# Sending each token's rows to their experts batch by batch, with scattered rows in place of gathered ones

## The reference, cut to what matters

```
logits = x @ gate_w.T                                   # 2048 x 64
topv, topi = jax.lax.top_k(logits, 8)
rw = jax.nn.softmax(topv)
W = jnp.zeros((N, E)).at[jnp.arange(N)[:, None], topi].set(rw)
gu = jnp.einsum('nh,eih->nei', x, gu_w)                 # gu_w 64 x 128 x 256
gate, up = gu[..., :64], gu[..., 64:]
inter_w = silu(gate) * up * W[:, :, None]
out = jnp.einsum('nei,ehi->nh', inter_w, dp_w)          # dp_w 64 x 256 x 64
out = out + sigmoid(x @ sh_gate1_w.T) * shared_expert(x)
```

## Time and profile before

| | |
|---|---|
| median of 3 runs | 1198.72 (1197.88 to 1201.56) |
| the profiled execution | 1203.47, its span 1201.7 |
| busy, PE / DVE / ACT / POOL | 907.1 / 869.8 / 567.8 / 520.3 |
| mean granted clock of TensorE | 0.895 |
| attention of layer 0 ends (last sum) | 143.55 |
| first gather for a unit, start of the last | 206.66, 446.72 |
| first and last gather of the return | 462.39, 630.09 |
| first work of the next block | 639.53 |

### The profile page before, as it was taken

The page is one execution under the profiler, slowest core; times in us unless marked ns, Lnnn a source line. Parts: engine busy times, 40 slices in busy tenths (PEclk is TensorE's granted clock), DMA queues, the critical chain, the costliest instruction groups (busy, mean ns, idle before and its releaser), DMA issues. The chain is left out here.

```text
span 1201.7 us, 16894 instructions
## 1 busy us (share of the span) xinstructions
PE 907.1 (75%) x5172; PEld 581.4 (48%) x5172; DVE 869.8 (72%) x2535; ACT 567.8 (47%) x1243; POOL 520.3 (43%) x532
## 2 busy tenths in 40 slices
PE   6899976888888884000007989999988899999887
PEld 5766744666666663000004433333322467688565
DVE  6467887599989873566445888878887569777465
ACT  3322267566666662000004366777768543434553
POOL 3100048777777764777774431111112144453000
PEclk9989985899999997555557999999999999999899
DMA  5060161677767765333332622222211300110001
GB/s 160 1 278 19 38 158 26 187 212 209 211 205 211 220 206 180 103 98 97 103 94 87 214 84 72 72 72 72 72 19 27 118 27 28 52 53 1 1 27 45
DMA packets 74522, 124.97 MB, mean 104 GB/s; under 512 B 12282, under 2 KB 52288, under 8 KB 73024
## 3 DMA queue, kind: packets, MB, share of 16 engines
q1 hardware_dynamic: 58944, 81.80, 22.3%
q0 software_dynamic: 15360, 41.96, 12.5%
q10 hardware_dynamic: 128, 0.13, 0.1%
HBM read 83.80 MB, written 35.66 MB: 99 GB/s over the span
## 5 line engine op out<-in xcount | busy, mean ns | idle before, releaser
L2026 DVE CUSTOM_DVE_ANT_0 masked<-ps,causal 128x128 f32<-128x128 f32 (+7 forms) x256 | 181.1, 755 | 40.7 <-PE ps L1825 39.7
L1539 POOL DMA_INDIRECT h_t<-modulated_rows,ga_rows x192 | 182.8, 952 | 60.8 <-issue 55.2
L145 PE MATMUL ps<-consts,xn 128*128 128x128 f32 x128 | 20.1, 308 | 177.1 <-PEq L78 104.2
L1551 POOL DMA_INDIRECT big<-expert_rows,slot x128 | 126.0, 984 | 55.2 <-issue 40.5
L2006 ACT ACTIVATE xn<-ps 128x512 f32<-128x512 f32 (+3 forms) x256 | 111.7, 511 | 43.6 <-PE ps L1847 42.7
L1458 DVE SCALAR_TENSOR_TENSOR xn<-big,weights,xn 128x256 f32<-128x256 f32 x128 | 62.5, 488 | 84.4 <-DMA big<-expert_rows,slot 80.4
L151 ACT ACTIVATE h_t<-ps,modc 128x512 f32<-128x512 f32 x24 | 17.4, 778 | 192.3 <-PE ps L145 97.9
L1130 PE MATMUL ps<-h_t,xn 128*128 128x128 f32 x768 | 104.9, 281 | 0.0
L145 PEld LDWEIGHTS ps<-consts,xn 128*128 128x128 f32 x128 | 16.8, 160 | 182.0 <-issue 109.9
L1130 PEld LDWEIGHTS ps<-h_t,xn 128*128 128x128 f32 x768 | 96.5, 197 | 0.9 <-issue 0.9
L1118 PE MATMUL ps<-consts,h_t 128*128 128x128 f32 x384 | 64.5, 292 | 35.9 <-DMA h_t<-modulated_rows,ga_rows 35.5
(11 more groups left out here) (321 smaller groups left out, 2184.4 us busy)
## 6 DMA issues: line engine op xcount, KB each, us to landing
expert_rows<-h_t SPq DMA_DIRECT2D x96, 256.0 KB, 2.6
qk<-qk_parts SPq DMA_DIRECT2D x72, 128.0 KB, 2.7
big<-in_gu SPq DMA_DIRECT2D x8, 1024.0 KB, 11.2
qk_parts<-parts SPq DMA_DIRECT2D x16, 384.0 KB, 2.6
raw<-in_mlp SPq DMA_DIRECT2D x16, 384.0 KB, 3.1
room<-in_down SPq DMA_DIRECT2D x4, 1024.0 KB, 10.7
h_t<-modulated_rows,ga_rows POOLq DMA_INDIRECT x192
h_t<-qk_parts SPq DMA_DIRECT2D x24, 128.0 KB, 2.7
```

The costliest lines, as they stand in the source:

```text
L1539: nc.gpsimd.indirect_dma_start(xg[:, u % 4, i, :], None, row_dram, bass.IndirectOffsetOnAxis(ap=idxg[:, 2 * u + i:2 * u + i + 1].bitcast(U ...
L1551: nc.gpsimd.indirect_dma_start(yg[:, t % 2, k, :], None, y_dram, bass.IndirectOffsetOnAxis(ap=slots[:, n:n + 1].bitcast(U32), axis=0))\
L2026: nc.vector.tensor_tensor_reduce(masked[:, at % 2, 0:k], ps[:, bank:bank + (k + GW - 1) // GW, :] .rearrange("p a n -> p (a n)")[:, 0:k], ...
```

## The change

- The capacity is now counted for each batch: 127 tiles, so 64 units a batch and 128 in all, where 96 were.
- Batch 0 is normalised, routed and given its slots inside batch 1's attention, at the tiles t = 8 to 12. TensorE's scores of t = 12 and t = 13 are no longer issued one tile ahead; those of 13 wait for the slots' keys.
- The list, its one-hot matrices and the gathers of L1539 go. POOL scatters instead (`send`): for each tile of tokens 8 indirect DMAs write the 128 rows from SBUF into their slots in `dispatched_rows`. A unit's 256 rows are then consecutive, and SP loads them with one plain DMA.
- Slots that no token has must hold finite numbers. SP fills `dispatched_rows` beforehand with 2 times 16 stores of 1 MB (`fill`), the first 16 in the projection block, the others in the attention.
- ACT takes over half of the unit's eviction, and the shared expert's output of batch 0.
- The rows of batch 0 are fetched and added while batch 1's units run (`combine_part`, 3 parts in 2 units); the return after the last unit has 8 tiles.

```diff
-SLOTS = (T * TOPK + E0 * (P - 1)) // P
-UNITS0 = (SLOTS + 1) // 2
+SLOTS = (SEQ * TOPK + E0 * (P - 1)) // P
+UB = (SLOTS + 1) // 2
+UNITS0 = BATCH * UB
...
+            FILLS = UB * 2 * P * D // (P * 2 * P * TOPK)
+            def fill(engine, b, rows_from):
+                rows = sent_dram[b * UB * 2 * P:(b + 1) * UB * 2 * P, :].rearrange("(n p r) d -> n p (r d)", n=FILLS, p=P)
+                for n in range(FILLS):
+                    engine.dma_start(rows[n], rows_from).then_inc(s_void[b], 16)
...
+            nothing = sb(projecting, "nothing", [P, 2 * P * TOPK])
...
+                    sp.wait_ge(s_clean, 1)
+                    fill(sp, 0, nothing[:, :])
                     sp.wait_ge(s_modd, 6)
                     sp.dma_start(mod_dram.rearrange("w b d -> b w d"),
...
+                    sp.wait_ge(s_wgu, 16 * 7)
+                    fill(sp, 1, big[:, 0:2 * P * TOPK])
...
+                    for i in range(UNITS0 + 7):
+                        if i < UNITS0:
+                            if i % UB == 0:
+                                all_sent(sp, i // UB)
+                            if i == 0:
+                                sp.wait_ge(s_shs, NG)
+                            if i >= 4:
+                                sp.wait_ge(s_t, i - 3)
+                            sp.dma_start(xg[:, i % 4, :, :],
+                                         sent_dram[i * 2 * P:(i + 1) * 2 * P, :].rearrange("(i p) d -> p i d", p=P))\
+                                .then_inc(s_xg[i % 4], 16)
+                        u = i - 7
+                        if u >= 0:
+                            sp.wait_ge(s_ye, u + 1)
+                            sp.wait_ge(s_yea, u + 1)
+                            sp.dma_start(y_dram[u * 2 * P:(u + 1) * 2 * P, :].rearrange("(i p) d -> p i d", p=P),
+                                         ys[:, u % 2, :, :]).then_inc(s_yst[u % 2], 16)
...
+                        if t in (8, 10):
+                            turned((t - 8) // 2)
+                        if t in (9, 11):
+                            logits((t - 9) // 2)
+                        if t == 11:
+                            scores(12)
+                        if t == 12:
+                            pe.wait_ge(s_cst, 2)
+                            count(0)
+                            pe.wait_ge(s_q, 1)
+                            ranks(0, ps[:, 3, :].rearrange("p (t e) -> p t e", t=TB), 0, TB)
+                            pe.wait_ge(s_key, 1)
+                            scores(13)
...
-                            nc.vector.tensor_copy(ys[:, u % 2, :, :],
-                                                  ps[:, 4 + 2 * (u % 2):6 + 2 * (u % 2), 0:D]).then_inc(s_ye, 1)
+                            nc.vector.tensor_copy(ys[:, u % 2, 0, :], ps[:, 4 + 2 * (u % 2), 0:D]).then_inc(s_ye, 1)
...
+                        u = i - 3
+                        if u >= 0:
+                            act.wait_ge(s_d, u + 1)
+                            if u >= 2:
+                                act.wait_ge(s_yst[u % 2], 16 * (u // 2))
+                            nc.scalar.copy(ys[:, u % 2, 1, :], ps[:, 5 + 2 * (u % 2), 0:D]).then_inc(s_yea, 1)
...
+                        late = i - UB - COMBINE_AT
+                        if late >= 0:
+                            for n in range(min(3 * late // 2, TB * PARTS), min(3 * (late + 1) // 2, TB * PARTS)):
+                                combine_part(n)
...
+                    def send(t):
+                        if t >= 2:
+                            pool.wait_ge(s_sent[t % 2], SENT * (t // 2))
+                        for n in range(t * TOPK, (t + 1) * TOPK):
+                            nc.gpsimd.indirect_dma_start(
+                                sent_dram, bass.IndirectOffsetOnAxis(ap=slots[:, n:n + 1].bitcast(U32), axis=0),
+                                xn[:, t, :], None).then_inc(s_sent[t % 2], 16)
...
+                    for t in range(NT):
+                        if t % TB == 0:
+                            pool.wait_ge(s_slot, t // TB + 1)
+                            pool.wait_ge(s_void[t // TB], 16 * FILLS)
+                        send(t)
+                        if t in (0, 3):
+                            ln_pool(pool, 1, (GB + t // 3,))
```

More of the change, by code:

```diff
@@ L1040, in tiles_of, with count @@
                     def tiles_of(t, n):
                         return bc(m16[:, t, :], 1, n)
-                    def bank(n):
-                        return ps[:, n, :].rearrange("p (t e) -> p t e", t=TB)
-                    def within(n, first):
-                        return nc.tensor.matmul(bank(n), tri16[:, :], m16[:, n * TB:(n + 1) * TB, :],
-                                                start=first, stop=False)
-                    def before(n):
-                        for t in range(TB - 1):
-                            nc.tensor.matmul(bank(n)[:, t + 1:, :], ones16[:, :], tiles_of(n * TB + t, TB - 1 - t),
+                    def count(b):
+                        pe.wait_ge(s_m, 2 * b + 2)
+                        out = ps[0:E0, 5 if b else 3, 0:1]
+                        for t in range(b * TB, (b + 1) * TB):
+                            last = nc.tensor.matmul(out, m16[:, t, :], ones16[:, 0:1], start=t == b * TB,
+                                                    stop=t == (b + 1) * TB - 1)
+                        last.then_inc(s_cnt, 1)
@@ L1057, in before, with ranks @@
+                    def ranks(b, out, first, n):
+                        nc.tensor.matmul(out, tri16[:, :], m16[:, first:first + n, :], start=True, stop=False)
+                        for t in range(b * TB, first):
+                            nc.tensor.matmul(out, ones16[:, :], tiles_of(t, n), start=False, stop=False)
+                        for t in range(n - 1):
+                            nc.tensor.matmul(out[:, t + 1:, :], ones16[:, :], tiles_of(first + t, n - 1 - t),
                                              start=False, stop=False)
+                        nc.tensor.matmul(out, q16[:, b, :], bc(later16[:, :], 1, n), start=False,
+                                         stop=True).then_inc(s_rank, 1)
@@ L1097, in _ @@
+                    pe.wait_ge(s_pta, len(hi_blocks))
+                    count(1)
                     shared(2)
+                    pe.wait_ge(s_q, 2)
+                    ranks(1, ps[:, 4, :].rearrange("p (t e) -> p t e", t=TB), TB, TB)
                     shared(3)
+                    for b in range(BATCH):
+                        last = nc.tensor.matmul(ps[0:E0, 5, 1 + b:2 + b], tri16[0:E0, 0:E0], q16[:, b, 0:1], start=True,
+                                                stop=True)
@@ L1167, in copied @@
                         for c in range(KC):
-                            last = nc.scalar.copy(h_t[:, c, g * GW:(g + 1) * GW], ps[:, T_BANK[g] + c, :])
+                            last = nc.scalar.copy(h_t[:, c, g * GW:(g + 1) * GW], ps[:, T_BANK[g][c], :])
                         last.then_inc(s_h, 1)
@@ L1246, in _ @@
                     act.wait_ge(s_tail, 16)
-                    for i in range(UNITS0 + 1):
+                    for i in range(UNITS0 + 3):
                         u = i
@@ L1272, in _ @@
                     nc.scalar.activation(c_row, c_row, ACT.Silu).then_inc(s_mod1, 1)
+                    for t in range(TB + 2, NT):
+                        shared_out(t)
                     act.wait_ge(s_modr, 2)
```

457 lines of the change are left out of this document (206 added, 251 removed).

## The result

The changed kernel takes 1223.3 us (median of 4 runs, 1219.2 to 1230.0) where the kernel before takes 1200.1 in the same comparison: 1.020 of it, 95% interval 1.014 to 1.026. It is slower, outside the range that was predicted and on the other side of no change. Its profiled execution is of 1219.2 with a span of 1217.5, 15.8 longer than the span before. It is the shortest of the four; the median stands 4.1 above it.

What follows compares the result with a forecast made beforehand. POOL's indirect DMAs were taken to bound loop and return, DVE close behind in the loop. 77 more for loop and start, 86 less for the return, 3 for the ends: 6 saved, 1192 us, range 1171 to 1212.

Steps and rivals of the forecast that it cites:

- From the median: 1198.7 - 6: Final step: 6 saved, taken from the old kernel's median, whose profiled execution stood 4.8 above it; 1192.7, say 1192.
- Routing inside attention, 19: Batch 0's routing ahead of attention's tile 13 adds 19; slots at about 134.5, attention ending near 160.
- Sends: Batch 0's 64 scatters on POOL at 1.257 each, 80.4, plus 3 for two `rstd` and a wait; first turn at 223.
- Fills, 0: The first 16 stores of 1 MB in the projection block take 39, done at 56, hidden, costing 0.
- The loop, 304.8: Expert loop of 128 units, first to last turn, summed over three paces to 304.8; last turn at 528.
- I take 2.45: Pace per unit while POOL sends batch 1, between 2.22 from DVE and 2.68 from DMA: 30.6 units in 75.
- 2.17 with POOL idle: Pace per unit once POOL's sends end, where TensorE's 2.11 binds: 33.4 units, 72.5.
- DVE 2.34 without POOL, 2.59 beside it ... I take 2.48: Pace per unit of batch 1's units carrying 80 combine parts, each part 0.52: 53.3 units, 132.2.
- The return, 105.5 from last turn to next block: After the last unit: first fetch at 540, 63 fetches at 1.30, landing and last sum; next block at 633.5.
- Nothing behind it changes.: Everything after the next block's start, 639.53 before, was taken as unchanged, so that start served as yardstick.
- queues bind: Rival, 0.24: while POOL issues DMAs, `ys` stores land late and ACT and DVE wait for the two buffers; 1204.
- The working's own signs of being wrong: Forecast wrong if batch 0's slots stand after 145 or before 125, or the mean pace lies outside 2.3 to 2.5.

Runs made afterwards that it cites:

- e25: The changed kernel with batch 0's count, ranks and slots after attention's last tile, batch 1's rstd ahead of the sends: 1235.1 us, 1.0314 of the kernel before.
- e10: The changed kernel with one semaphore per batch for the sends, so no send waits for earlier ones: 1214.2 us, 1.0128 of the kernel before.
- e23: e19 plus a third `ys` buffer, and the shared expert's multiplication and batch 0's 64 weights on DVE ahead of the first unit: 1186.7 us, 0.988 of the kernel before.
- e26: The changed kernel with DVE's wait for a part moved to just before the next part: 1213.1 us, 1.0108 of the kernel before.
- e22: The changed kernel with only parts 0 and 9 of each tile's sum left in the loop: 1210.1 us, 1.0083 of the kernel before.
- e19: The changed kernel with the deferred part wait, one semaphore per batch, and ScalarE copying both tiles from unit 72 on: 1204.1 us, 1.0046 of the kernel before.

## Why the prediction was wrong, step by step

The working gave 1197.5 for the profiled execution (1203.5 less 6) and 1219.2 was measured, 21.7 more: 9.9 up to the first turn (forecast 223), 6.9 in the loop, under 1 in the return and 4.5 behind it, to rounding. The step "From the median: 1198.7 - 6" adds another 9. It supposed that the new profiled execution would stand 4.8 above its median too, and it stands 4.1 below; that is the spread of executions, which the working did not reckon with, and no cost of the change. No one step carries the 21.7. The largest is the price of a unit with parts, and it is the step that failed.

- *Routing inside attention, 19.* Slots were forecast at 134.5 and stand at 138.3. The attention's end moved from 143.6 to 165.2, by 21.7; by the working's own 19 it would be 162.5, where the text says "near 160". The mechanism is right, the size some 3 to 4 short. e25 shows that the step pays 13 in this kernel.
- *Sends.* 1.257 each was right (1.265). The sentence "64 sends are 80.4, two `rstd` and a wait for group 2's statistics 3" left out that a send waits for sends two tiles back: 5.3 at 188 us. The wait is in the diff and was put at nothing without a reason. e10 gives it back. With the 3.8 of the slots it makes nearly the whole 9.9.
- *Fills, 0.* Right: the write of the modulation rows is at 59.90, before at 59.81.
- *The loop, 304.8.* Measured 311.7: up to the turn of unit 64 148.2 (forecast 147.5), for the next eight 18.0 (21.4), and from unit 72 to the last turn 145.6 (135.9). "I take 2.45" for the sends was too high (2.28 on the trace, and 2.13 in e23: DMA engines at a share of 1.00 moved 324 to 342 GB/s, more than the 300 that I had scaled from the earlier trace rows); 2.17 with POOL idle was right (2.19). "DVE 2.34 without POOL, 2.59 beside it ... I take 2.48" is the step that failed, by 9.7: a part was priced at 0.52, from a row of eight in which only parts follow on parts, and the wait behind it, ahead of the next unit's copies, was not. A lone part takes 1.01. The pace was 2.58 to 2.65; e26 takes 13.4 from the loop by moving the wait. And 5 went at 318 to 323 where POOL and DVE compute at once, a place that the working passed over; it ate what the faster sends had given.
- *The return, 105.5 from last turn to next block.* Right: 106.25.
- *"Nothing behind it changes."* Wrong by 4.5, and in every variant: the rest is 565.7 to 567.0 in all eight profiles of this scheme on chips of this kind and 561.7 to 562.2 in both of the old one. A part of it shows in the first 50 us of layer 1. TensorE's first product of the causal part stood 25.8 behind the start of the block, and now 28.4, since the q and k rows come back later (their first load is issued 18.6 behind the block's start instead of 15.9, though the stores ahead of it start 9.2 to 9.3 behind it in both):

```profile
665.34 0.33 PE L1825 MATMUL ps<-qk 96*128 96x128 bf16 x2 [0.54 <-ACT v_ones L1978]
```

```profile
679.26 0.33 PE L1879 MATMUL ps<-qk 96*128 96x128 bf16 x2 [2.57 <-DMA qk<-qk_parts]
679.42 1.81 PE L1941 MATMUL ps<-h_t,swap 128*128 128x512 f32 x2
```

The first row is of the kernel before. Behind that wait of 2.57 the granted clock falls (0.93 in the stretch 671 to 681, 0.95 in the next 20 us, 1.00 in both before), and the same two matmuls take 1.81 instead of 1.06. Why the rows come back later is open, and no experiment moved this term.

Of the rivals, "queues bind" named the right place and the wrong rank: the two `ys` buffers were the second bound, hidden behind DVE in the changed kernel and shown only by e22 and e23. Its time, 1204, was nearer than the forecast and still short. The working's own signs of being wrong did not show: the slots stand between 125 and 145, and the mean pace, 311.7 over 127 units, is 2.45 and inside 2.3 to 2.5. Both have wide bounds for one term each, and the miss is a sum over several. The sign of the forecast hung on 77 more for loop and start against 86 less for the return, a margin of 6 in 1200, with the added costs made of many small steps and the saving of one large, certain one. Each missed wait could only go one way. That the first 64 units came out at 148, within 1 of the forecast, is luck: sends that were faster than forecast, and the halt at 319 that was not in it, cancel.

## What to carry to other kernels

Price the waits that a change adds as well as its work: a wait for one's own last instruction holds up everything behind it in that queue, and here moving it gave as much as leaving out most of the work. When one bound is removed and half the gain is missing, look at who waits now; the second bound was one buffer away, and with both removed TensorE came to its own pace (the buffer alone was not tried). And when a saving is certain and the costs are a sum of small steps, expect the sum to be short, not the saving.

## What the runs showed of the hardware

- On two of the chips TensorE stood still for up to 20 us at a time while POOL issued indirect DMAs, with the DMA engines at a share of 0.32; the kernel before took 1260 there and this scheme 1342 to 1361 (medians), whatever was edited. The gathers of the kernel before have it in a milder form: in the run with 128 units the pace is 3.03 there (1372 matmuls in 260 us) against 2.50. A comparison needs the kernel before from the same chip.
- Loads, stores and scatters of 1 KB pieces together moved 342 GB/s at a share of 1.01 (e23, above). The fill, stores of 1 MB in 8 KB pieces, and the loads ahead of it moved 426 GB/s at the same share. The limit of about 358 GB/s that the Trainium skill gives a core (DMA: Bandwidth & Descriptors, Specifications) is not borne out for this stretch, which is 426. The stretch of the changed kernel:

```profile
20.00:40.00 20.00, 18.58 (x112) 16.25 (x112) 16.51 (x43) 7.89 (x12) 6.77 (x4) 1.00 1.01 426
```

- A scatter of 128 rows costs POOL what a gather does: median 0.96 and 0.30 between.
- Beside a POOL multiplication of 1.27, DVE's copy of two small tiles took 2.63 instead of 0.59. The Trainium skill, GPSIMD Engine Reference, Specifications, has the two engines share an SBUF interface for DVE instructions in a two-port mode or with two inputs from SBUF; the trace agrees, in these numbers, for a `scalar_tensor_tensor` with two inputs from SBUF (1.30 instead of 0.28). For the copy it shows the delay; whether the copy runs in such a mode no run here shows. In e19 the same two take 1.28 and 2.62 beside POOL's multiplication, and in e23, without it, the copies take 0.59.
